# A fused attention and gated-FFN layer on one core: squares of low parts on TensorE, integer weights on SyncE's queue, the first Q stack in two halves

## The chip, the cores and the metric

One core of a Trainium2 chip runs the whole layer for 16 batches in one launch. The metric is the device time of the launch in microseconds. The engines are named as in the profile: PE is TensorE (PEld its weight load), DVE is VectorE, ACT is ScalarE, POOL is GpSimd and SP is SyncE, which here only issues DMAs. A time with a decimal point and no unit is a time in us from the start of the span.

## The reference, cut to what matters

For each of 16 batches (x is 256 queries by 256 channels, ctx 120 rows by 256, 16 heads of depth 16):

```python
def layernorm(x): return (x - mean(x)) / sqrt(var(x) + 1e-5)
Q, K, V = layernorm(x) @ Wq.T + bq, ctx @ Wk.T + bk, ctx @ Wv.T + bv
scores  = einsum('bhqd,bhkd->bhqk', Q, K) * 0.25 / temperature
x = x + einsum('bhqk,bhkd->bhqd', softmax(scores), V) @ Wo.T + bo
n = layernorm(x)
h = silu(n @ (w_gate / 127).T) * (n @ (w_up / 127).T)      # integer weights, hidden 768
x = x + h @ (w_down / 127).T
```

## The kernel before, in words

The kernel keeps float32 accuracy on a matrix engine that rounds its inputs: each operand is a high part and a low part, and a product is three matmuls, high by high, low by high and high by low. Q and K are split into three bf16 parts (high, middle, lowest), and the six products that matter are put below one another as 96 rows of one tile, the Q stack `qs` and the K stack `ks`. SP builds a stack by six DMAs of 16 rows each from the parts that ACT (high, `highest` L509; middle, `middle` L515), DVE (the rest, `rest_of` L636) and POOL (lowest, `third` L457) make; `stack` (L358) issues them. The A group (L894) is the score product from which DVE takes row maxima (`max`, L704); the maxima are transposed (`shift`, L818) and go as two more rows into the Q stack (`shift rows`), and the B group (L904) then gives transposed scores with the maximum subtracted, which ACT exponentiates (L536). `pv` (L920) multiplies by V. Then come the normalisation by row sums, the output product `wo`, the second layernorm, six gate-up products and two down products.

The integer weights are loaded as int32 into the buffers of `y`, `x1` and `x_res`, before these are in use. ACT rounds them into the high part (`integer_weight`, L493), DVE makes the low part (L667). For weights that fit, the low part is all zero, and the products with it are skipped. Whether that is so is found at run time: `look_for_wide` (L417) squares and adds the three low parts on POOL in 512-column pieces, with nine multiplications and eight additions, and halves the sum three times; `tell_if_wide` (L670) reduces it on DVE, a one-column matmul (L883) adds over partitions, DVE writes the answer to a register word (`told`), and PE reads it (`read`). The first `pv` waits for the answer too.

The order of work on each engine is written out beforehand. Time is cut into steps, 32 for a batch. `JOBS` gives PE's work with the step and the PSUM bank, `LAG` all other kinds, `EVERY` the distance of the parts of one kind, `START` work that is done once, and `SHIFT` moves a kind in one batch. Every engine walks through the steps in order and emits what is due; a step takes no time of its own, so only the order on each engine counts, and semaphores do the rest. `WARM` puts matmuls of the identity with itself between PE's work in the head (L880). Every engine runs its own program in order: an instruction that waits holds all behind it, and a DMA issued by SP stands behind every earlier wait of SP. The first layernorm's mean and variance are on DVE (`stats1`, `var1`), its reciprocal root on POOL (`rsqrt`, L439), its application on ACT (`norm_apply`, L521). `ctx` is split into parts by ACT (`ctx hi`) and POOL (`ctx lo`, L474) for two batches at a time, and K is computed for two batches at a time.

Of the kernel before, what the change touches and what calls it, by code (L numbers as in the profile page):

```python
# [13 lines left out]
P = 128  # L14
RING = 3
# [6 lines left out]
    ("k", 0, -59, 3),  # L22
    ("normT1", 0, -56, 1),
    ("q", 0, -51, 1),
    ("v", 0, -45, 0),
    ("shift", 0, 9, 2),
    ("attQ", 0, 56, 3),
    ("attQ", 1, 56, 1),
    ("attT", 0, 61, 3),
    ("wo", 0, 69, 0),  # L30
    ("normT2", 0, 84, 2),
    ("gateup", 0, 87, 2),
    ("gateup", 1, 89, 0),
    ("gateup", 2, 93, 1),
    ("gateup", 3, 97, 2),
    ("gateup", 4, 104, 3),
    ("gateup", 5, 106, 0),
    ("down", 0, 113, 3),
    ("down", 1, 118, 1),
# [7 lines left out]
    "A": -22, "max": -19, "load x_res": -11, "shift rows": -1, "bias x_res": 4, "shift hi": 10, "shift lo": 13,  # L47
    "exp": 21, "B": 21, "pv": 34, "pv copy": 37, "rsum": 57, "att": 58, "attT hi": 62,
    "attT lo": 64, "x1": 72, "stats2": 73, "rsqrt2": 74, "var2": 74, "norm2": 82, "normT2 hi": 83,
    "normT2 lo": 85, "tanh": 88, "gate": 89, "hid": 90, "hid hi": 92, "hid lo": 94, "hid lo last": 111,  # L50
    "y": 117, "store": 157,
}
EVERY = {
    "rsum": 1, "k rows": 4, "q rows": 1, "exp": 4, "A": 4, "B": 4, "max": 4, "pv": 16, "pv copy": 15,
# [5 lines left out]
    "load wv": -115, "load wo": -57, "load bv": -124, "load bo": -29, "weight q": -64, "weight o": -30,  # L60
    "weight v": -42, "ones rows": -44, "load wg": -70, "load wu": -65, "load wd": -73, "int hi": (-42, -26, -24),
    "int lo": (-36, -29, -20), "look": (-30, -26, 6), "tell": 31, "sum": 36, "told": 32, "read": 68,
# [4 lines left out]
    "A": {3: -1, 15: -2},  # L67
    "B": {1: -1},
    "att": {1: -3},
    "attQ": {0: 3, 1: -2},  # L70
    "attT": {0: 3},
    "attT hi": {0: 2},
    "ctx hi": {0: -2},
    "ctx lo": {0: -10, 2: -9},
    "exp": {1: -2},
    "hid lo": {14: 3},
    "k rest": {2: 1},
    "k rows": {2: 1},
    "max": {15: -1},
    "norm1": {3: -5},  # L80
    "normT1": {3: -4},
    "normT1 hi": {3: -4},
    "normT2": {14: -2},
    "pv": {0: 2},
    "pv copy": {1: -1},
    "q mid": {1: 7},
    "q rest": {0: 5},
    "q rows": {2: -3},
    "q third": {15: -17},
    "rsqrt2": {15: -3},  # L90
    "rsum": {1: -4},
    "shift lo": {0: -1, 1: -2},
    "stats1": {2: -6},
    "stats2": {0: 1},
    "wo": {14: -3},
    "x1": {1: 1},
# [47 lines left out]
def build(nc, x, ctx, wqT, bq, wkT, bk, wvT, bv, woT, bo, temp, tempc, wgT, wuT, wdT, out):  # L144
# [27 lines left out]
    with es:  # L172
# [72 lines left out]
        WIDE_LEFT = 64  # L245
        wide_one = tanh_g[:].rearrange("p a q -> p (a q)")
        WIDE_STEPS = 3 * 6 - 1 + 3
# [16 lines left out]
        ks_in = [sem(f"ks_in{r}") for r in range(RING)]  # L264
        shift_in = [sem(f"shift_in{r}") for r in range(RING)]
# [7 lines left out]
        wide_got, wide_all, wide_col, wide_sum, wide_set = sem("wide_got"), sem("wide_all"), sem("wide_col"), sem("wide_sum"), sem("wide_set")  # L273
# [56 lines left out]
        def _(sp):  # L330
# [27 lines left out]
            def stack(kind, n, part, t, dst, arrived, parts):  # L358
# [4 lines left out]
                for r in range(len(parts)):  # L363
                    if parts[r] == part:
                        sp.dma_start(dst[n % RING][r * D:(r + 1) * D], src).then_inc(arrived[n % RING], 16)

            def step(i):
                if i == START["load wv"]:
                    load_weight("v", wvT)
                if i == START["load wo"]:  # L370
                    load_weight("o", woT)
                if i == START["load bv"]:
# [33 lines left out]
        def _(pool):  # L406
# [10 lines left out]
            def look_for_wide(k):  # L417

                pool.wait_ge(gint_lo, k + 1)
                flat = (wg, wu, wd)[k][:, 1].bitcast(F32).rearrange("p c n -> p (c n)")  # L420
                done = 6 * k - (k > 0)
                for part in range(3):
                    piece = flat[:, part * 512:(part + 1) * 512]
                    if k + part == 0:
                        nc.gpsimd.tensor_tensor(wide_sq, piece, piece, ALU.mult).then_inc(wide_got, 1)
                        done += 1
                        continue
                    pool.wait_ge(wide_got, done)
# [537 lines left out]
```

## Time and profile before

| what | value |
|---|---|
| median of 3 runs | 418.03 us (417.88 to 419.41) |
| the profiled execution's own time | 417.83 us |
| its span, first to last instruction | 415.70 us |
| mean granted TensorE clock | 0.967 of full speed |
| PE busy | 376.0 us, 90% of the span |
| DVE, ACT, POOL busy | 299.0, 254.5, 183.0 us |
| chain that ended last, by engine | PE 73%, POOL 11%, DMA, ACT and DVE 4% each |

The share of an engine is over the whole span; the head (until TensorE is busy without a break), the steady turns and the tail have to be read apart. The chain is followed back from the last instruction, at each step to what released it.

### The profile page before, as it was taken

Reading aid. Unit: us, or ns where it says so; the run is one execution under the profiler, and the core shown is the slowest. Engines: PE = TensorE matmul, PEld = TensorE weight load, DVE = VectorE, ACT = ScalarE, POOL = GpSimd, SP = SyncE. Lnnn points to the kernel's source line nnn. Section 1 sums busy time; section 2 is a strip of 40 time slices with the busy share of each in tenths; the row PEclk is TensorE's granted clock in tenths of the full one; section 3 lists DMA queues with packets and bytes.
Section 4 is the critical chain, followed back from the end, with each engine's and each line's share of the span. In section 5 each row is a group of like instructions: output and inputs, shape, how many; then the busy total and the mean of one; then the engine's idle time right before and its main releaser. Section 6 shows DMA issues by size and latency. Waiting matters only on the chain.

```text
span 415.7 us, 9912 instructions
## 1 busy us (share of the span) xinstructions
PE 376.0 (90%) x3492; PEld 338.6 (81%) x3492; DVE 299.0 (72%) x733; ACT 254.5 (61%) x564; POOL 183.0 (44%) x302
## 2 busy tenths in 40 slices
PE   7359567979999999999999999999999999997985
PEld 6359545758998999998999999999999988786974
DVE  6388272678878788778777877787778785745664
ACT  2422244757677767767766766676767665756442
POOL 3139993415544445345452635353444332514223
PEclk9859895999999999999999999999999999999999
DMA  6955445657371737262736264645535451010000
GB/s 149 304 74 129 63 100 102 125 84 115 74 122 41 114 94 120 75 120 75 132 76 123 69 128 87 105 88 114 102 79 90 88 78 54 3 54 2 27 25 27
DMA packets 61700, 37.69 MB, mean 91 GB/s; under 512 B 34000, under 2 KB 61136, under 8 KB 61648
## 3 DMA queue, kind: packets, MB, share of 16 engines
q1 hardware_dynamic: 60320, 34.63, 43.6%
q10 hardware_dynamic: 1328, 2.36, 1.7%
q8 instruction: 33, 0.54, 0.6%
q14 instruction: 19, 0.16, 0.2%
HBM read 14.04 MB, written 4.19 MB: 44 GB/s over the span
## 4 chain that ended last, share of the span: by engine, by line
PE 73%; POOL 11%; DMA 4%; ACT 4%; DVE 4%; issue 2%; SPq 1%; POOLq 0%; ACTq 0%; DVEq 0%
PE ps_w L799 30%; PE ps_w L792 10%; PE ps_o L920 7%; PE ps_b L904 7%; PE ps_a L894 6%; PE ps_w L811 5%; PE ps_w L784 4%; PE ps_w L832 3%; POOL hid L431 3%; DMA x_tok<-x 3%; POOL tanh_g L429 2%; POOL hidT L452 2%; DMA qs<-q 1%; DVE ks L689 1%; ACT xn L521 1%
## 5 line engine op out<-in xcount | busy, mean ns | idle before, releaser
L452 POOL TENSOR_TENSOR hidT<-hid,hidT 128x256 fp32r<-128x256 f32 x80 | 59.0, 738 | 130.5 <-ACT hidT L529 130.5
L799 PE MATMUL ps_w<-xn2T,wg 128*128 128x256 f32 x384 | 102.3, 300 | 0.3 <-DVE xn2T L629 0.2
L704 DVE TENSOR_REDUCE negmax<-ps_a 128x4 f32<-128x480 f32 x128 | 82.7, 650 | 19.9 <-PE ps_a L894 19.9
L799 PE MATMUL ps_w<-xn2T,wu 128*128 128x256 f32 x384 | 95.6, 281 | 0.0
L536 ACT ACTIVATE probs<-ps_b 120x512 f32<-120x512 f32 x128 | 76.1, 594 | 26.6 <-PE ps_b L904 26.3
L799 PEld LDWEIGHTS ps_w<-xn2T,wg 128*128 128x128 f32 x384 | 72.3, 188 | 1.5 <-DVE xn2T L629 0.7
L799 PEld LDWEIGHTS ps_w<-xn2T,wu 128*128 128x128 f32 x384 | 72.6, 189 | 0.0
L799 PE MATMUL ps_w<-wd,hidT 128*128 128x256 f32 x384 | 55.9, 292 | 2.8 <-DVE hid L764 1.5
L547 ACT ACTIVATE tanh_g<-ps_w 128x256 f32<-128x256 f32 x96 | 36.6, 382 | 34.4 <-PE ps_w L799 33.8
L904 PE MATMUL ps_b<-qs,ks 98*120 98x256 bf16 x256 | 51.0, 281 | 3.9 <-ACT probs L536 3.9
L894 PE MATMUL ps_a<-ks,qs 96*128 96x120 bf16 x512 | 49.0, 219 | 4.7 <-DMA qs<-q 3.8
L799 PEld LDWEIGHTS ps_w<-wd,hidT 128*128 128x128 f32 x384 | 48.3, 189 | 5.4 <-DVE hid L764 1.9
L529 ACT ACTIVATE hidT<-hid 128x256 fp32r<-128x256 f32 x96 | 39.7, 414 | 10.7 <-DVE hid L764 10.1
L760 DVE SCALAR_TENSOR_TENSOR hid<-tanh_g,ps_w 128x256 f32<-128x256 f32 x96 | 39.2, 409 | 7.4 <-ACT tanh_g L547 5.4
L894 PEld LDWEIGHTS ps_a<-ks,qs 96*128 96x128 bf16 x512 | 31.8, 99 | 12.2 <-DMA qs<-q 4.3
L764 DVE TENSOR_TENSOR hid<-hid,ps_w 128x256 f32<-128x256 f32 x96 | 39.5, 412 | 1.9
L904 PEld LDWEIGHTS ps_b<-qs,ks 98*120 98x120 bf16 x256 | 27.5, 135 | 12.1 <-issue 6.2
L920 PE MATMUL ps_o<-probs,v_one 120*32 120x256 f32 x512 | 35.1, 393 | 0.6 <-ACT probs L536 0.5
L792 PE MATMUL ps_w<-xn1T,wq 128*128 128x256 f32 x192 | 27.5, 293 | 0.4 <-DVE xn1T L629 0.4
L629 DVE TENSOR_TENSOR xn2T<-ps_w,xn2T 128x512 fp32r<-128x512 f32 x16 | 11.1, 692 | 21.8 <-ACT xn2T L498 21.8
L784 PE MATMUL ps_w<-wv,ctxT 128*120 128x256 f32 x96 | 16.2, 306 | 11.0 <-DVE wv L600 11.0
L792 PE MATMUL ps_w<-wo,attT 128*128 128x256 f32 x192 | 26.0, 284 | 0.0
(94 smaller groups left out, 659.0 us busy)
## 6 DMA issues: line engine op xcount, KB each, us to landing
qs<-q SPq DMA_DIRECT2D x96, 128.0 KB, 4.6
ks<-k SPq DMA_DIRECT2D x96, 60.0 KB, 2.7
x_tok<-x SPq DMA_DIRECT2D x16, 256.0 KB, 3.7
x_res<-x SPq DMA_DIRECT2D x16, 256.0 KB, 3.9
out<-y SPq DMA_DIRECT2D x16, 256.0 KB, 3.2
ctx_raw<-ctx SPq DMA_DIRECT2D x16, 120.0 KB, 2.5
x_res<-wdT ACTq DMA_DIRECT2D x1, 768.0 KB, 9.0
y<-wgT ACTq DMA_DIRECT2D x1, 768.0 KB, 10.9
```

Of the source, the lines that this page charges most:

```text
L452: nc.gpsimd.tensor_tensor(hidT[:, 1, f], hid[:, f % 2], hidT[:, 0, f].bitcast(F32), ALU.subtract).then_inc(hid_lo, 1)
L529: nc.scalar.activation(hidT[:, 0, f], hid[:, f % 2], ACT.Copy).then_inc(hi["hid"], 1)
L536: nc.scalar.activation(probs[0:NKV, e % PROBS], ps_b[0:NKV], ACT.Exp).then_inc(exp_done, 1)
L547: nc.scalar.activation(tanh_g[:, f % 2], bank_of("gateup", f)[:, 0:NQ], ACT.Tanh, scale=DEQ / 2).then_inc(tanh_done, 1)
L704: nc.vector.tensor_reduce(negmax[:, n % RING, qt, h0:h0 + AG], ps_a[ga % 2][:, 0:AG * NKV].rearrange("p (h k) -> p h k", h=AG), AX.X, ALU. ...
L760: nc.vector.scalar_tensor_tensor(hid[:, f % 2], tanh_g[:, f % 2], 1.0, ps[:, 0:NQ], ALU.add, ALU.mult).then_inc(gated_done, 1)
L764: nc.vector.tensor_tensor(hid[:, f % 2], hid[:, f % 2], ps[:, NQ:2 * NQ], ALU.mult).then_inc(emptied["gateup"], 1)
L792: last = nc.tensor.matmul(dst, lhsT, rhs, start=(k == 0 and one is sums[0]), stop=(k == len(one) - 1), skip_group_check=True)
L799: last = nc.tensor.matmul(dst, lhsT, rhs, start=(start and k == 0), stop=(stop and k == len(terms) - 1), skip_group_check=True)
L894: last = nc.tensor.matmul(ps_a[ga % 2][:, k * NKV:(k + 1) * NKV], qs[n % RING][0:KS_ROWS, h0 + k, qt * P:(qt + 1) * P], ks[n % RING][0:KS_ ...
L904: last = nc.tensor.matmul(ps_b[0:NKV, k * NQ:(k + 1) * NQ], ks[n % RING][:, gb * HG + k], qs[n % RING][:, gb * HG + k], start=True, stop=True)
L920: last = nc.tensor.matmul(ps_o[k % HQ * VW:(k % HQ + 1) * VW, k // HQ], v_one[n % RING][:, h], probs[0:NKV, count(n, GROUPS, h // HG) % PR ...
```

## The change

- `look_for_wide` on POOL goes. In its place PE multiplies each 128-column piece of the three low parts with itself and adds all 36 products in one PSUM tile; the diagonal holds sums of squares. They are issued in six pieces of six. DVE multiplies the tile by the identity and takes the maximum of each row (L672 and what follows, as before).
- The filler matmuls (`WARM`) go.
- The three integer weights are loaded from SP's queue, each in two halves (by chunks), in place of ACT's queue.
- For batch 0 each of the six Q rows is sent as two DMAs of 128 queries, the first with a semaphore of its own, `qs_half_in`; the A groups of the first 128 queries (four of eight) wait for that one alone.
- The step tables are written anew: nearly all lags move by six steps, which changes no order by itself; kinds move against each other by one to nine steps in all batches, and by more in batches 0 to 3 and 13 to 15. The second transpose goes from bank 2 to bank 3, the first down product from bank 3 to bank 2. On POOL the residual's bias (`bias x_res`) goes from between the low parts of the hidden tile to behind the second layernorm's root.

```diff
-    ("normT2", 0, 84, 2),
+    ("normT2", 0, 89, 3),
-    ("down", 0, 113, 3),
+    ("down", 0, 119, 2),
...
-    "A": -22, "max": -19, "load x_res": -11, "shift rows": -1, "bias x_res": 4, "shift hi": 10, "shift lo": 13,
+    "A": -16, "max": -13, "load x_res": -6, "shift rows": 14, "shift hi": 16, "shift lo": 19, "bias x_res": 24,
...
-    "weight v": -42, "ones rows": -44, "load wg": -70, "load wu": -65, "load wd": -73, "int hi": (-42, -26, -24),
-    "int lo": (-36, -29, -20), "look": (-30, -26, 6), "tell": 31, "sum": 36, "told": 32, "read": 68,
+    "weight v": -51, "ones rows": -133, "load wg": (-57, -50), "load wu": (-47, -46), "load wd": (-42, -40), "int hi": (-46, -29, -21),
+    "int lo": (-36, -25, -18), "squares": (-20, -19, -15, -14, -11, -9), "tell": -3, "sum": 2, "told": 7, "read": 61,
...
+    "norm1": {0: -44, 1: -4, 3: -15},
+    "q mid": {0: 7, 1: -2, 2: 1, 3: 2, 13: -2, 15: -3},
+    "q rows": {0: -3, 1: 4, 2: 6, 3: 5, 13: -4, 15: -3},
+    "q third": {0: -5, 1: 4, 2: 3, 3: -2, 13: -1, 14: 6, 15: 4},
+    "rsqrt1": {0: -70, 1: 4, 3: -3, 13: 8},
+    "var1": {0: -64, 1: -2, 2: -5, 3: -12},
...
-WARM = {-59: 10, -56: 2, -51: 5, -40: 12, -24: 4, -22: 18, -18: 2, -14: 2, -10: 2, -6: 2, -2: 2, 2: 2, 6: 2}
-FIRST, LAST = -142, TURN * (BATCHES - 1) + 204
+FIRST, LAST = -225, TURN * (BATCHES - 1) + 235
...
+            def load_integers(k, half):
+                w, chunks, arrived = ((wgT, CC, gate_in), (wuT, CC, up_in), (wdT, FC, down_in))[k]
+                part = slice(half * chunks // 2, (half + 1) * chunks // 2)
+                sp.dma_start(raw_int[k].rearrange("p (c n) -> p c n", c=chunks)[:, part], w.rearrange("(c p) n -> p c n", p=P)[:, part]).then_inc(arrived, 16)
...
-                    if parts[r] == part:
+                    if parts[r] == part and kind == "q" and n == 0:
+                        for half in range(QT):
+                            sp.dma_start(dst[0][r * D:(r + 1) * D, :, half * P:(half + 1) * P], src[:, :, half * P:(half + 1) * P]).then_inc(qs_half_in if half == 0 else arrived[0], 16)
+                    elif parts[r] == part:
...
+                if kind == "q" and n == 1:
+                    act.wait_ge(qs_half_in, 6 * 16)
...
-                dve.wait_ge(wide_got, WIDE_STEPS)
-                nc.vector.reduce_max(wide_any[:], wide_sq[:, 0:WIDE_LEFT], AX.X).then_inc(wide_all, 1)
+                dve.wait_ge(wide_squares, 6)
+                dve.wait_ge(ident_done, 2)
+                nc.vector.tensor_tensor(wide_sq[:, 0:P], ps_o[:, 0, 0:P], ident[:], ALU.mult).then_inc(wide_diag, 1)
+                dve.wait_ge(wide_diag, 1)
+                nc.vector.reduce_max(wide_any[:], wide_sq[:, 0:P], AX.X).then_inc(wide_all, 1)
...
+            def squares_of_low_parts(piece):
+                w = (wg, wu, wd)[piece // 2][:, 1].rearrange("p c n -> p (c n)")
+                pe.wait_ge(gint_lo, piece // 2 + 1)
+                for k in range(6):
+                    part = w[:, (piece % 2 * 6 + k) * P:(piece % 2 * 6 + k + 1) * P]
+                    last = nc.tensor.matmul(ps_o[:, 0, 0:P], part, part, start=(piece == 0 and k == 0), stop=(piece == 5 and k == 5), skip_group_check=True)
+                last.then_inc(wide_squares, 1)
...
+                    if ga == 0 and n == 0:
+                        pe.wait_ge(qs_half_in, 6 * 16)
+                    if ga == (GROUPS // QT if n == 0 else 0):
+                        pe.wait_ge(qs_in[n % RING], slot_count(n, 1, 1) * (6 * 16))
```

## Rows read from the trace of the kernel before

**Rows 1.** Busy by stage: stretch, length, PE, PEld, DVE, ACT, POOL, clock, DMA, GB/s.
```profile
37.00:48.00 11.00, 6.99 (x74) 6.75 (x72) 6.29 (x15) 1.96 (x4) 10.39 (x9) 1.00 0.58 90
60.00:72.00 12.00, 8.52 (x56) 5.53 (x57) 4.71 (x11) 5.34 (x10) 5.53 (x10) 0.58 0.64 117
186.70:229.55 42.85, 42.85 (x424) 39.19 (x428) 34.25 (x89) 30.69 (x72) 19.72 (x35) 1.00 0.51 99
```

**Rows 2.** TensorE's waits, 37 to 100: total us, times, longest.
```profile
PE ps_w L784 <- POOL ctxT L474: 4.2, 1, 4.2
PE ps_a L894 <- DMA qs<-q: 3.8, 2, 2.6
PE ps_w L811 <- ACT xn L521: 2.9, 1, 2.9
```

**Rows 3.** Busy by stage for POOL alone: stretch, length, busy, clock, DMA, GB/s.
```profile
30.08:46.85 16.77, 15.92 (x11) 0.96 0.69 120
51.90:60.87 8.97, 8.34 (x9) 1.00 0.41 92
```

**Rows 4.** Timeline of PE: start, us, what; the score groups that open batches 0 to 3.
```profile
37.19 0.38 PE L894 MATMUL ps_a<-ks,qs 96*128 96x120 bf16 x4
...
54.45 0.38 PE L894 MATMUL ps_a<-ks,qs 96*128 96x120 bf16 x4 [1.24 <-DMA qs<-q]
...
69.83 0.60 PE L894 MATMUL ps_a<-ks,qs 96*128 96x120 bf16 x4
...
87.59 0.38 PE L894 MATMUL ps_a<-ks,qs 96*128 96x120 bf16 x4 [2.57 <-DMA qs<-q]
```

**Rows 5.** Groups of DVE, 0 to 40: busy, mean ns, idle before.
```profile
L689 DVE MEMSET ks<- 2x1920 bf16 x3 | 5.0, 1658 | 1.2 <-issue 1.2
```

**Rows 6.** Timeline of several engines: durations that the sum uses.
```profile
5.75 0.43 SPq L335 DMA_DIRECT2D probs<-wvT  x1
...
7.68 2.89 PE L784 MATMUL ps_w<-ctxT,wk 128*128 128x240 f32 x12 [1.52 <-POOL ctxT L474]
...
9.20 1.09 ACT L521 ACTIVATE xn<-x_tok,norm_bias,rstd 128x256 f32<-128x256 f32 x2 [3.02 <-POOL norm_bias L447]
...
13.14 1.66 PE L792 MATMUL ps_w<-xn1T,wq 128*128 128x256 f32 x12 [0.39 <-DVE xn1T L629]
...
17.06 1.48 ACT L493 ACTIVATE wg<-y 128x1536 fp32r<-128x1536 int32 x1 [0.89 <-DMA y<-wgT]
...
24.73 0.28 POOL L442 TENSOR_TENSOR minus_mean<-zero_col,meanvar 128x2 f32<-128x2 f32 x1 [7.39 <-DVE meanvar L648]
...
26.34 0.20 POOL L447 TENSOR_TENSOR norm_bias<-minus_mean,rstd 128x2 f32<-128x2 f32 x1
...
27.23 1.16 POOL L457 TENSOR_TENSOR q<-q_rest,q 128x512 bf16<-128x512 f32 x1 [0.70 <-ACT q L515]
27.88 2.13 DVE L667 TENSOR_TENSOR wg<-y,wg 128x1536 fp32r<-128x1536 int32 x1
...
32.51 3.88 SPq L365 DMA_DIRECT2D ks<-k  x6
...
49.37 1.16 POOL L457 TENSOR_TENSOR q<-q_rest,q 128x512 bf16<-128x512 f32 x1
...
70.59 2.41 PE L792 MATMUL ps_w<-xn1T,wq 128*128 128x256 f32 x12
```

**Rows 7.** DMA issues, whole span: count, KB each, median us to landing.
```profile
qs<-q SPq DMA_DIRECT2D x96, 128.0 KB, 4.6
ks<-k SPq DMA_DIRECT2D x96, 60.0 KB, 2.7
```

**Rows 8.** Groups of PE by form, whole span.
```profile
L880 PE MATMUL ps_o<-ident 128*128 128x128 f32 x130 | 21.6, 329 | 1.5 <-POOL ident L409 1.5
```

**Rows 9.** Chain that ended last, in order of time: start, us, what.
```profile
341.94 1.37 POOL x_res L480 x2
```

**Rows 10.** TensorE's waits, 330 to 416.
```profile
PE ps_w L811 <- ACT xn L521: 2.5, 3, 1.2
```

More of the change, by code:

```diff
@@ L63 @@
+    "int lo": (-36, -25, -18), "squares": (-20, -19, -15, -14, -11, -9), "tell": -3, "sum": 2, "told": 7, "read": 61,
 }
 SHIFT = {
[L67 to L82, printed above, removed]
@@ L83 @@
-    "normT2": {14: -2},
-    "pv": {0: 2},
[L85 to L96, printed above, removed]
-}
-WARM = {-59: 10, -56: 2, -51: 5, -40: 12, -24: 4, -22: 18, -18: 2, -14: 2, -10: 2, -6: 2, -2: 2, 2: 2, 6: 2}
-FIRST, LAST = -142, TURN * (BATCHES - 1) + 204
+    "A": {0: 5, 1: 1, 3: -1, 15: -3},
@@ new lines @@
+    "B": {0: -2},
+    "attQ": {13: -1},
+    "attT": {0: 1, 13: 2, 14: 3, 15: -2},
+    "attT hi": {0: -1, 3: -1, 13: 2, 14: 3, 15: 1},
+    "attT lo": {1: 3, 2: -2, 13: 3, 14: -1},
+    "bias x_res": {0: -16, 1: 17, 2: 4, 13: 10},
+    "ctx hi": {0: -53, 1: 17, 2: -2, 3: -3, 13: 6},
+    "ctx lo": {0: -60, 1: -20, 2: -8, 3: 13, 13: 8},
+    "down": {14: -2, 15: 15},
+    "exp": {0: -1, 1: -1, 13: 1},
+    "gate": {15: 23},
+    "hid": {2: 1, 13: 1, 15: 25},
+    "hid hi": {14: 2, 15: 23},
+    "hid lo": {0: -1, 1: -1, 3: -1, 13: -10, 14: -2, 15: 3},
@@ new lines @@
+    "hid lo last": {14: 6, 15: 31},
[6 rows of a table added]
+    "load ctx": {0: -62, 1: -16, 2: -9, 3: -20, 13: 11},
+    "load x": {0: -70, 1: -6, 2: -26, 3: -31, 13: 2, 14: -16},
+    "load x_res": {0: 13, 2: 8, 13: 18, 15: -13},
+    "max": {0: 1, 1: -1, 2: -1, 15: -2},
[18 rows of a table added]
+    "rsum": {13: -1},
+    "shift": {0: 2, 1: -1, 2: 2, 13: 2},
+    "shift hi": {0: 9, 1: 1, 2: 1, 3: 2, 13: 1},
+    "shift lo": {2: 2, 13: 1},
+    "shift rows": {0: 9, 1: -1, 2: -4, 13: 3, 14: 6, 15: 6},
+    "stats1": {0: -91, 1: -29, 2: -8, 3: -13, 13: -2},
@@ L371, in step @@
                     load_weight("o", woT)
+                for k, name in enumerate(("load wg", "load wu", "load wd")):
+                    if i in START[name]:
+                        load_integers(k, START[name].index(i))
                 if i == START["load bv"]:
@@ L415, in _ @@
             pool.wait_ge(consts_done, 1)
[L417 to L428, printed above, removed]
-                    nc.gpsimd.tensor_tensor(wide_one, piece, piece, ALU.mult).then_inc(wide_got, 1)
-                    pool.wait_ge(wide_got, done + 1)
-                    nc.gpsimd.tensor_tensor(wide_sq, wide_sq, wide_one, ALU.add).then_inc(wide_got, 1)
-                    done += 2
-                if k == 2:
-                    for half in (256, 128, 64):
-                        pool.wait_ge(wide_got, done)
-                        nc.gpsimd.tensor_tensor(wide_sq[:, 0:half], wide_sq[:, 0:half], wide_sq[:, half:2 * half], ALU.add).then_inc(wide_got, 1)
-                        done += 1
             def rsqrt(which, n, got, eps_sem, out_sem, norm_sem):
@@ L716, in step @@
                     dve.wait_ge(emptied["wo"], count(n, 1, 1))
+                    at_least(dve, var2, count(n - 1, 1, 1))
                     norm_stats(1, x1[:, n % RING], n, stats2)
@@ L722, in step @@
                     dve.wait_ge(x_in[n % RING], slot_count(n, 1, 1) * 16)
+                    at_least(dve, var1, count(n - 1, 1, 1))
                     norm_stats(0, x_tok[:, n % RING], n, stats1)
@@ L876, in _ @@
             wide = []
+            def squares_of_low_parts(piece):
[5 more added lines that the diff above has]
+                last.then_inc(wide_squares, 1)
             def step(i):
-                for _ in range(WARM.get(i, 0)):
-                    nc.tensor.matmul(ps_o[:, 1, 0:P], ident[:], ident[:], start=True, stop=True)
+                if i in START["squares"]:
+                    squares_of_low_parts(START["squares"].index(i))
                 if i == START["sum"]:
                     pe.wait_ge(wide_col, 1)
-                    nc.tensor.matmul(ps_o[0:1, 0, 0:1], wide_any[:], ones_col[:], start=True, stop=True).then_inc(wide_sum, 1)
+                    nc.tensor.matmul(ps_o[0:1, 1, 0:1], wide_any[:], ones_col[:], start=True, stop=True).then_inc(wide_sum, 1)
                 if i == START["read"]:
```

71 lines of the change are left out of this document (34 added, 37 removed), and 24 rows, old and new, of tables (LAG, SHIFT).

## The prediction

> **What bounds the kernel now.** I read the busy table by stages first, because a share over the whole span mixes three regimes. In two steady turns, 186.70 to 229.55, TensorE is busy for all of their 42.85 us at the full granted clock [rows 1]: 21.43 us a batch, and sixteen of them would be 342.8 us. The span is 72.9 us longer, and that lies before the steady part and behind it. No edit that only reorders engines other than TensorE can gain anything in between. In the head TensorE works 6.99 of 11.00 us and 8.52 of 12.00 us [rows 1], and the first of these stretches includes matmuls on the identity (L880) that compute nothing.
>
> Then I asked whom TensorE waits for in the head [rows 2]: 4.2 us for the low part of ctx, which POOL makes, 3.8 us for Q stacks to land, 2.9 us for ACT's normalisation, which in turn needs POOL's reciprocal root. The third view shows what POOL does then: the scan for wide weights holds it from 30.08 to 46.85 and again from 51.90 to 60.87, 24.3 us of work in 20 instructions [rows 3]. POOL works in program order, so the ctx low part, the root for batch 2 and the third part of Q for batch 1 stand behind the first scan, and the third part of K and the root for batch 3 behind the second. The head is bound by a scan that nobody needs before the first PV product. TensorE's milestones set the scale [rows 4]: first score groups of batches 0 to 3 at 37.19, 54.45, 69.83 and 87.59.
>
> **The change, part by part.** I add up the profiled execution, span 415.70, its own time 417.83 (2.13 us around the span; the median of the runs, 418.03, is 0.2 above it).
>
> *Start until the first score group.* The three memsets of ones rows move from between Q's high part and Q's rest to ahead of the first variance. They are 5.0 us of work with 1.2 us before them, 6.2 us in all [rows 5]. So the first normalisation on ACT, at 9.20 before, starts near 9.2 + 6.2 = 15.4, some 0.4 sooner because POOL's root now stands ahead of the ctx low part: 15.0. It takes 1.09, the transposes, copies and the K product follow in a row (2.89 us for K's twelve matmuls at their slow first speed) and K's high part is out near 20.5. Then ACT has the first integer weight (1.48), K's middle part and Q's high part (to 23.5), the second integer weight (to 25.0); DVE makes the first low part (2.13) and then the second batch's variance, near 24.4. POOL's root takes 1.8 (24.73 to 26.54 in the row), ACT's normalisation of batch 1 ends near 27.3, and only then comes Q's middle part (to 27.9), since ACT has it behind that normalisation. POOL's third part takes 1.16: 29.1, against 28.39 before (durations and starts in [rows 6]). The memsets thus gain nothing here: what they free at Q's rest is spent at the front.
>
> Then SyncE's queue. An issue of such rows costs 0.65 us (3.88 for six), one of a weight 0.43 [rows 6], and batch 0 has twelve Q issues in place of six: 3.9 us more of queue. In order from 20.5: three of K, two weights, two of K, one weight (near 25.0), six of Q's high part (29.0; its middle part has been ready for a us), four of the middle part, one of K, and the first half of the lowest part, out near 32.8. A half is 64 KB in runs of 256 bytes; no such transfer is in the trace. The nearest row is K's, 60 KB in runs of 240 bytes, 2.7 us; the whole Q rows take 4.6 [rows 7]. Nothing makes a half slower than the whole, so 2.7 to 4.6; I take 3.3, near K's. Scores of batch 0 start near 36.1, 1.1 us earlier than 37.19. The halves are issued alternately, so the early semaphore saves only the last issue, 0.65 us, and the wait for the second half is hidden behind the four groups before it.
>
> Here the skill has a rule against the change: the Trainium skill, "DMA: Bandwidth & Descriptors", section "Rules for kernel authors", advises against cutting one transfer in two, since both halves go through the same engines, and its section "Specifications" wants 512 bytes or more in a transfer for full rate. K's rows agree in part: a 240-byte transfer of half the size takes more than half the time. By the rule a pair of halves costs 2 x 2.7 - 4.6 = 0.8 us more than a whole, and the forecast would be 408.8.
>
> The integer weights move to SyncE's queue, six issues in place of three on ACT. Four of them and two of x sit before the K rows, while SyncE has nothing else to do until 20.5; hidden. The two of the last weight and the output weight stand between K's and Q's rows, 3 x 0.43 = 1.3 us, and 1.1 of it is on the path above, since Q's middle part comes at 27.9 and the queue is free at 29.0. What stays tied to them is the low part of the last weight, which the fifth squares piece needs ahead of the first scores: the load is out near 25.0, down 4 us later by Q's row, then ACT 1.48 and DVE 2.13, so 32.7. That is 3.4 us before 36.1: covered.
>
> *Squares on TensorE.* 36 matmuls of 128x128. The identity matmuls of that shape are 130 instructions, two for each, 21.6 us [rows 8]. Bounds: 0.06 us each, half of a 256-column matmul in the Q product (1.66 for twelve [rows 6]), or 0.33, two identity instructions as they overlapped; 2 to 12 us in all. I take 0.14 for each, the row per column nearest to it in type: 5 us. Four of six pieces run while TensorE waits for DVE; two, 1.7 us, lie around the first scores and the first Q product of batch 1. They replace 65 identity matmuls, so TensorE's load falls. DVE gains one product over 128 columns, between 0 and 1 us (POOL's over 512 columns take 1.16), and a sum of it is not late: the second batch's Q stack, not the last maxima, releases that batch. The telling is done by 45, well ahead of the first PV.
>
> *POOL free.* This is the gain. The ctx low part of batch 2 now waits for its load (SyncE issues it near 34) and ACT: near 39.6, instead of after the first scan's end at 46.85 [rows 3]. The third part of Q for batch 1 ends near 42.6 instead of 50.53 (its row starts at 49.37), so its stack lands near 47.8, and the first scores of batch 1 start 6.7 us earlier than 54.45 [rows 4, 6]. From there the path is Q product, high, rest, middle (ACT has two exponentials first), third, 0.65 issue, 4.6 landing: batch 2's scores near 62.3, 7.5 earlier. The root for batch 3, which stood behind the second scan's end at 60.87, is done by 51, so the 2.9 us wait for ACT goes too. What is late next is again the Q stack, behind the exponentials on ACT. For batch 3 I get 77.8 (9.8 earlier), as the order puts its third part behind only the ctx low part and one root. From then on TensorE has gate-up work to fill every wait, as in the steady row. Head: 9.8 us; I take off 1.3 for semaphore hops not counted and for the first matmuls without filler: 8.5.
>
> *Steady turns.* Kinds move by one or two places. The bank of the second transpose goes to 3 and that of the down product to 2: the gate-up product must now wait for the first y. It is covered by the second down half (twelve matmuls, as Q's 1.66) with PV, V and a transpose besides, against one short DVE instruction. I take 0, from -1 to +10.
>
> *Tail.* The residual's bias moves from between the low parts to behind the root: 1.37 us of POOL leaves the path twice (at 341.94, and again one turn on [rows 9]), but TensorE waits only 2.5 us for that normalisation in three places, one of them 1.2 [rows 10]. So the two give back at most 2.5 - 1.2 = 1.3: I take 1.3.
>
> Sum: 417.83 - 8.5 - 1.3 = 408.0.
>
> **Rivals.**
> 1. *TensorE's clock without filler.* In the stretch from 60 to 72, behind a 2.9 us wait, the granted clock is 0.58 (1.2 GHz for most of it), and twelve Q matmuls take 2.41 against 1.66 us [rows 1, 6]. The change removes all 65 filler matmuls, which also stand in the gaps between batch 0's score groups, where the clock was 1.00. For it: the gaps stay. Against: the maxima on DVE, not TensorE, pace the scores. I count some 38 us of dense work (the two full Q, K, V and score sets and half a turn of gate-up) between 36 and 92; at 1.45 times (2.41 / 1.66) that is 17 us more, of which the idle 18 us hide most. Three tenths on the path give back 5: 413. The skill's rule stands beside it: the Trainium skill, "TensorE: Matmul & The Clock Gate", Part 1, says the throttled state is the default and only activity lifts it; the row of 60 to 72 agrees.
> 2. *SyncE's queue takes POOL's place.* Twelve halves, K rows, shift rows and loads stand in one in-order queue; each wait there holds all behind it. If a Q or shift issue of batches 1 and 2 comes 3 us late each, 6 are lost: 414. For it: 3.8 us of stack waits already [rows 2]. Against: all twelve halves are out by 33.5, before batch 1 needs the queue.
> 3. *Slower: the exchanged banks stall every turn.* Place: the gate-up product behind the first y, in 14 turns. From 0.7 us a turn the gain is gone (14 x 0.7 = 9.8); at 1.1 it is 423.4. For it: steady turns have no slack on TensorE at all [rows 1]. Against: the cover named above.
>
> **How the numbers follow.** Forecast 0.57 (own range 402 to 412), clock 0.18, queue 0.14, banks 0.06, anything else 0.05. The low end, 400.0, has two thirds of the scan's 24.3 us leave the path (16.2) with the tail's 1.3; the high end, 415.5, takes in rivals 1 and 2 and the upper bound of the squares (7 us more, of which a fifth lies on the path). Half a per cent, 2.1 us, is about what can be told from no change. Faster 0.87 (forecast, clock, most of queue, part of the rest), same 0.05, slower 0.08 (banks and part of the rest).
>
> **What would show it.** Right: POOL's scan rows gone and the third part of batch 1's Q before 44; first scores near 36, 48, 62 and 78; steady pairs of turns still 42.85; the first two waits for ACT's normalisation in the tail gone. Wrong: scores of batch 0 later than 38 (squares or queue), slow matmuls past 60 (clock), any TensorE wait in a steady turn (banks), Q stack waits over 6 us in the head (queue).

## The result and the profile after

The changed kernel takes 415.53 us (median of 20 runs, 412.63 to 418.87) against 418.25 for the kernel before (20 runs, 413.95 to 421.13). The ratio is 0.9945, 95% interval 0.992 to 0.9969: faster by half a per cent, 2.3 us by the ratio, where 10 had been forecast. The profiled execution took 413.98 us (span 412.2); the forecast was set against 417.83, so 3.85 us came where 9.83 were expected.

The busy table by stages, columns as in [rows 1], the first and last of its stretches again and one between them:

```profile
37.00:48.00 11.00, 7.38 (x60) 6.75 (x60) 4.58 (x13) 3.85 (x8) 3.60 (x6) 0.75 1.01 136
60.00:72.00 12.00, 9.43 (x93) 7.18 (x92) 5.13 (x10) 5.71 (x12) 1.04 (x1) 0.87 0.79 110
186.70:229.55 42.85, 42.85 (x424) 39.17 (x424) 34.44 (x88) 30.89 (x70) 19.41 (x34) 1.00 0.56 106
```

The steady part is what it was, TensorE busy for all of 42.85 us. POOL's scan is gone; the same stretches as in [rows 3], for POOL alone:

```profile
30.08:46.85 16.77, 3.50 (x6) 0.63 1.17 117
51.90:60.87 8.97, 4.65 (x8) 0.69 0.51 99
```

POOL's work there fell from 24.3 to 8.2 us. The last two figures of a line are the share of the DMA engines and GB/s: in the first stretch the share rose from 0.69 to 1.17 while the rate stayed (120, now 117). The share adds up the times of all packets; above 1, packets of one engine overlap in time. Now the score groups that open batches 0 to 3, as in [rows 4]:

```profile
39.24 0.58 PE L919 MATMUL ps_a<-ks,qs 96*128 96x120 bf16 x4 [3.46 <-DMA qs<-q]
...
52.29 0.58 PE L919 MATMUL ps_a<-ks,qs 96*128 96x120 bf16 x4 [1.87 <-DMA qs<-q]
...
67.34 0.38 PE L919 MATMUL ps_a<-ks,qs 96*128 96x120 bf16 x4 [1.42 <-DMA qs<-q]
...
84.63 0.39 PE L919 MATMUL ps_a<-ks,qs 96*128 96x120 bf16 x4 [2.60 <-DMA qs<-q]
```

All four wait for a Q stack. Batch 0 starts 2.05 us later than before, batches 1 to 3 start 2.16, 2.49 and 2.96 earlier; the second PV half of batch 2 starts at 98.16 (100.92 before). So the head gives 2.76 us, the rest of the span 0.74 and the time around the span 0.35, in all 3.85.

TensorE's waits from 37 to 100 (total, times, longest), and then the one from 320 on that answers to [rows 10]:

```profile
PE ps_a L919 <- DMA qs<-q: 9.3, 4, 3.5
PE ps_a L919 <- DVE negmax L716: 2.2, 3, 1.4
```
```profile
PE ps_w L825 <- ACT xn L536: 0.4, 1, 0.4
```

The waits for POOL's ctx and ACT's normalisation in [rows 2] are gone; the waits for Q's landing went from 3.8 to 9.3 us. The chain of waits of the changed kernel tells where batch 0's stack comes from (start, us, what; a DMA's time counts from the start of its issue):

```profile
14.62 1.10 ACT xn L536 x2
...
19.29 0.82 ACT k L524 x2
20.13 0.71 SPq L399
...
31.89 0.62 SPq L399
32.55 6.64 DMA qs<-q
39.24 0.58 PE ps_a L919 x4
```

From 20.13, when K's high part is out, SyncE issues without a pause until 33.83. The third part of Q is ready at 27.96 and its halves are issued at 32.55 and 33.2: it stands almost five us in the queue, and then takes over six to land.

### The profile page after: what moved, and what is told of

Its sections match the earlier page's. It is cut to its first block, busy times and chain, and to the rows that moved or that the text cites. A ratio compares the mean times of both kernels' runs of the same rounds, so it can differ in the third digit from the quotient of the medians.

```text
span 412.2 us, 9745 instructions
## 1 busy us (share of the span) xinstructions
PE 363.0 (88%) x3398; PEld 326.1 (79%) x3398; DVE 299.6 (73%) x734; ACT 255.7 (62%) x564; POOL 157.4 (38%) x282
## 4 chain that ended last, share of the span: by engine, by line
PE 74%; DMA 8%; SPq 5%; POOL 4%; ACT 4%; DVE 3%; issue 2%; POOLq 0%; ACTq 0%; DVEq 0%
PE ps_w L813 30%; PE ps_w L806 10%; PE ps_o L945 7%; PE ps_b L929 6%; PE ps_a L919 6%; DMA qs<-q 6%; PE ps_w L798 5%; PE ps_w L825 5%; PE ps_w L846 3%; SPq L399 3%; DMA x_res<-x 2%; SPq L397 1%; ACT probs L551 1%; DVE ks L701 1%; POOL hidT L467 1%
## 5 line engine op out<-in xcount | busy, mean ns | idle before, releaser
L919 PE MATMUL ps_a<-ks,qs 96*128 96x120 bf16 x512 | 50.2, 222 | 12.5 <-DMA qs<-q 10.1
L919 PEld LDWEIGHTS ps_a<-ks,qs 96*128 96x128 bf16 x512 | 30.8, 100 | 21.0 <-DMA qs<-q 11.2
L825 PE MATMUL ps_w<-ident,xn 128*128 128x128 f32 x128 | 20.8, 288 | 16.2 <-ACT xn L536 16.2
L487 POOL TENSOR_TENSOR ctxT<-ctx_raw,ctxT 128x480 fp32r<-128x480 f32 x8 | 9.7, 1216 | 51.7 <-ACT ctxT L590 51.7
L806 PE MATMUL ps_w<-xn1T,wq 128*128 128x256 f32 x192 | 29.2, 305 | 0.0
L825 PEld LDWEIGHTS ps_w<-ident,xn 128*128 128x128 f32 x128 | 15.0, 147 | 17.5 <-issue 17.5
```

Of the source, the lines that this page charges most:

```text
L806: last = nc.tensor.matmul(dst, lhsT, rhs, start=(k == 0 and one is sums[0]), stop=(k == len(one) - 1), skip_group_check=True)
L825: last = nc.tensor.transpose(ps[:, c * NQ + t * P:c * NQ + (t + 1) * P], src[:, t, c * P:(c + 1) * P], ident[:])
L919: last = nc.tensor.matmul(ps_a[ga % 2][:, k * NKV:(k + 1) * NKV], qs[n % RING][0:KS_ROWS, h0 + k, qt * P:(qt + 1) * P], ks[n % RING][0:KS_ ...
```

## Experiments

Each ratio is to the kernel before, run on the same chip; the changed kernel's own is 0.9945 (0.992 to 0.9969).

**Whole rows, clock, memsets, scan alone.** Theory: batch 0's halves and SyncE's queue ate the gain. Rivals: the clock without filler; the memsets at the front; a scan that was worth less than forecast.

*e1: whole Q rows in batch 0, as before the change.*

```
-  if parts[r] == part and kind == "q" and n == 0: (two halves)
-  elif parts[r] == part:
+  if parts[r] == part:
```

> The changed kernel with the Q rows of batch 0 sent whole (six DMAs, one semaphore), all else as changed. Theory Q (the stack of batch 0 is late because twelve halves double the packets and the issues in the DMA queue): first scores at 36.0 to 37.5 in place of 39.24, DMA share above 1.2 for some 6 us less, the ctx load of batch 2 lands some 2 us sooner, and the time falls by 1.5 to 3 us to some 413. Rival C (TensorE's low clock took the gain): first scores may come sooner, but the Q product of batch 1 still takes 2.9 us and the time changes by less than 0.5 us. The prediction's own step (a half lands as fast as a K row, 3.3 us): first scores 0 to 1 us later than with halves.

413.12 us, ratio 0.9879 (0.9845 to 0.9912). First scores at 36.15 and 47.99, 3.1 and 4.3 earlier than in the changed kernel. The halves cost 0.7% as sent. The end of batch 0's chain in this run:

```profile
29.40 6.70 DMA qs<-q
36.10 0.05 issue
36.15 0.38 PE ps_a L912 x4
```

The last whole row takes as long to land as the last half did (6.70 and 6.64). The gain lies in the issue: with six issues fewer it goes out at 29.40 in place of 32.55.

*e2: identity matmuls in the head's waits.* 39 of them, into a bank that is free.

```
+  for _ in range(k):
+      nc.tensor.matmul(ps_b[:, 0:P], ident[:], ident[:], start=True, stop=True)
```

> The changed kernel with filler matmuls of the identity put back into TensorE's waits of the head (24 ahead of the third squares piece and of the first scores, 15 between the later score groups up to batch 1's second). Theory C (low clock): the Q products of batches 1 and 2 fall from 2.91 to 1.7 us, first scores of batch 1 at 51 and of batch 2 at 65 to 66, the time falls by 1.5 to 2.5 us. Theory Q (DMA queue): the two Q products are faster but first scores stay at 39.2, batch 1's fall by no more than 1.2 and the time by 0 to 1 us.

414.58 us, 0.9898 (0.9872 to 0.9923), at most half a per cent from the changed kernel, with intervals that touch. The stretch from 24 to 56 of the changed kernel, then of this one (columns as in [rows 1]):

```profile
24.00:56.00 32.00, 19.14 (x126) 17.57 (x125) 18.25 (x36) 9.08 (x17) 8.76 (x15) 0.63 1.06 133
```
```profile
24.00:56.00 32.00, 22.61 (x210) 21.08 (x208) 18.57 (x37) 9.98 (x19) 9.16 (x16) 1.00 1.06 133
```

The granted clock went from 0.63 to 1.00, the twelve matmuls of batch 1's Q product from 2.91 to 1.68 us, and the first scores of the four batches came at 39.54, 52.29, 66.62 and 84.61: nowhere as much as one us earlier. The clock was low, and it was not on the path to the first scores of these batches. Whether the half per cent in the total is real, and where it would come from, is not shown.

*e3: the memsets of ones rows late.*

```
-  "ones rows": -133
+  "ones rows": -13
```

> The changed kernel with the three memsets of ones rows moved from ahead of the first variance to where DVE is idle before the first maximum (step -13). Start theory (the chain from the first layernorm to SyncE's rows is on the path, memsets and all): ACT's first normalisation at 9 instead of 14.6, K rows issued from 14.5 instead of 20.1, first scores 3 to 5 us earlier than 39.24 and the time 2 to 4 us lower. Rival (what is late is the load of the last integer weight and the squares that stand ahead of the first scores, or DMA packets): first scores at most 1 us earlier, time within 1 us.

409.02 us, 0.9771 (0.9738 to 0.9803): 1.7%, 7.3 us, better than the changed kernel. Its chain and its first score group:

```profile
8.21 1.10 ACT xn L536 x2
...
14.02 0.71 SPq L399
```
```profile
30.95 0.39 PE L919 MATMUL ps_a<-ks,qs 96*128 96x120 bf16 x4 [1.75 <-DMA qs<-q]
```

Set beside the chain above, the normalisation moves by 6.4 us, K's first row on the queue by 6.1, the first scores by 8.3.

*e4: before, with only the scan replaced by the squares* (and nine of the eighteen filler matmuls at their place taken out).

```
-  if i in START["look"]: look_for_wide(...)
+  SQUARES = {-22: (0, 1), -18: (2,), -14: (3,), -10: (4,), -6: (5,)}
```

> The kernel before with one part of the change alone: POOL's scan replaced by the squares on TensorE and the diagonal on DVE, the fillers ahead of the first scores halved from 18 to 9, tables otherwise as before (whole Q rows, integer weights on ACT's queue). The prediction's theory (the scan is what bounds the head): batch 1's first scores near 47, the time 6 to 9 us below before. Theory Q (behind the scan SyncE's queue and the stacks' landing come next): the ctx low part at 41 to 43 in place of 46.9, batch 1's first scores at 49 to 51, the time 2 to 4 us below before. If it is as fast as the changed kernel, the other parts of the change gave nothing together.

414.70 us, 0.9874 (0.9832 to 0.9915). First scores at 37.09, 50.04, 65.01 and 83.17, against [rows 4] 0.1, 4.4, 4.8 and 4.4 earlier. This one part gives more than the whole change; the others together cost 0.7%, with the nine fillers counted to the scan.

**POOL's order, and the queue's load.** In the changed kernel POOL waits long for the residual's load, ahead of a root:

```profile
53.91 1.42 POOL L493 TENSOR_TENSOR x_res<-x_res,bo_row 128x256 f32<-128x256 f32 x2 [6.96 <-DMA x_res<-x]
```

*e5: that bias later.*

```
-  "bias x_res": {0: -16, 1: 17, 2: 4, 13: 10}
+  "bias x_res": {0: 17, 1: 17, 2: 4, 13: 10}
```

> The changed kernel with one place moved: POOL adds batch 0's residual bias behind the root of batch 3 and the low part of batch 2's K, where it stood ahead of them and waited 7.0 us for its load. Theory 'POOL's order': the wait holds everything behind it on POOL, so batch 2's scores come up to 2.5 us earlier than 67.3 and batch 3's 2 to 4 us earlier than 84.6; total 1 to 3 us less than the changed kernel. Theory 'stacks' (SyncE's queue and the landing of Q decide each batch): scores move less than 1 us, total within 0.8 us of the changed kernel.

415.68 us, 0.9983 (0.995 to 1.0015): no gain. The third part of batch 2's Q starts at 59.56 (59.88 in the changed kernel), as it waits for ACT's middle part:

```profile
59.56 1.16 POOL L472 TENSOR_TENSOR q<-q_rest,q 128x512 bf16<-128x512 f32 x1 [3.89 <-ACT q L530]
```

The wait for the residual stands on the chain of waits, but another stands right behind it that ends nearly as late. 'POOL's order' falls. The program up to batch 0's first scores is the changed kernel's here, and they came at 38.48 in place of 39.24: differences of that size between two profiles say nothing.

*e7: integer weights on ACT's queue.*

```
-  sp.dma_start(raw_int[k]..., part)
+  act.dma_start(raw_int[k]..., part)
```

> The changed kernel with the six loads of integer weights back on ACT's queue. Theory 'issues' (the queue in program order is the limit): three issues of 0.5 to 0.65 us go from between K's and Q's rows, first scores 1 to 2 us earlier than 39.2, total 0.5 to 2 us less. Theory 'short runs' (the DMA engines are the limit while 240 and 256-byte runs are moved): the last half still lands near 39, total within 0.8 us of the changed kernel.

418.98 us, 1.0046 (1.0011 to 1.0082): slower, which neither theory had. On ACT the issues stand behind its own waits: the first four, out by 9.67 on SyncE, come between 19.61 and 21.45, when K's rows go out too. The last weight's two halves then take 8.9 us to land (median), K's rows pause on SyncE (22.72, then 26.05), and the first scores come at 43.56. The move to SyncE, at these places in the order, is worth 1.0%.

**Why the halves land late.**

*e8: batch 0's halves by rows of the stack.*

```
-  dst[0][r*D:(r+1)*D, :, half*P:(half+1)*P], src[:, :, half*P:(half+1)*P]
+  dst[0][r*D + half*D//2 : r*D + (half+1)*D//2], src[half*P//2 : (half+1)*P//2]
```

> The changed kernel with the twelve Q issues of batch 0 cut by rows of the stack, not by queries: as many issues and the same bytes, but runs as long as those of the whole rows; the scores then wait for all twelve. Theory 'short runs': 64 KB land in 3 to 4.6 us in place of 6.6, first scores at 36.5 to 37.5, total 2 to 4 us less. Theory 'issues': twelve issues end where they did (33.8), landing 4 us or more, first scores at 38 or later, total within 1 us of the changed kernel.

416.40 us, 0.9975 (0.9933 to 1.0017). First scores at 41.89 with a wait of 5.89 us: long runs alone do not help. It is no clean test, though: the share of the DMA engines from 28 to 36 is only 0.65 to 0.69 while the stack lands later than in the changed kernel, so part of the engines seem to have had no work from it.

*e11: halves by heads.*

```
+  dst[0][r*D:(r+1)*D, half::CC], src[:, half]
```

> The changed kernel with the twelve Q issues of batch 0 cut by heads, not by queries: as many issues and the same bytes, in runs of 512 bytes over all sixteen rows of a part; the scores wait for all twelve. Theory 'packets' (256-byte runs double the packets, and a packet costs the engines about the same): share of the DMA engines from 28 to 36 us near 1.2 in place of 1.4, landing 4 to 5 us after the last issue at 33.8, first scores near 38.2, total 0.5 to 1.5 us less than the changed kernel. Theory 'issues': first scores at 39 or later, as with halves by queries.

414.01 us, 0.9917 (0.9885 to 0.9949). As many issues, ended at 33.82, and first scores at 36.37: as with whole rows (36.15), whose last issue ended at 30.03. The issues are those of the changed kernel, so the 2.9 us are landing alone; that is more than 'packets' had forecast. Whole rows and halves by heads come to the same time by different ways: six issues fewer with 6.7 us to land, or twelve issues with 3.1 for the last. In the total this run cannot be told from the changed kernel.

*e9: output weight and last integer weight loaded early.*

```
-  "load wo": -44, "load wd": (-42, -40)
+  "load wo": -49, "load wd": (-48, -47)
```

> The changed kernel with the loads of the output weight and of the last integer weight ahead of K's rows on SyncE's queue, into the stretch from 16 to 20 us in which the DMA engines move nothing. Theory 'burst' (Q's rows come late because weights, K's rows and Q's rows all pass the DMA engines between 22 and 38 us): 1.0 MB leaves that burst, three issues of 0.5 to 0.6 us leave the queue, first scores at 35 to 37.5 in place of 39.2, total 2 to 4 us less than the changed kernel. Theory 'packets' (the 256-byte runs alone keep the engines busy): Q's last issues end 1.2 to 1.7 us sooner, first scores at 37.5 to 38.5, total 1 to 2 us less.

412.26 us, 0.9877 (0.9823 to 0.9931). First scores at 36.01, as 'burst' had it. The first half sent lands in 3.1 us; in the changed kernel, behind the last integer weight, it took 5.7.

*e13: all first halves ahead of all second halves; nothing else.*

```
-  for half in range(QT):
-      sp.dma_start(... half * P:(half + 1) * P ...)
+  sp.dma_start(... 0:P ...)
...
+  if kind == "q" and n == 0 and part == 2:
+      for r in range(len(parts)):
+          sp.dma_start(... P:2 * P ...)
```

> The changed kernel with one thing moved: batch 0's six first halves ahead of its six second halves, where the change sends both halves of a row one behind the other; as many issues, bytes and runs of 256 bytes. Theory 'same rows' (two transfers to the same sixteen rows at once slow each other): DMA share from 28 to 36 us at 0.6 or less in place of 1.4, halves land in 2.7 to 3.5, first scores at 33 to 36. Theory 'burst' (weights and rows together fill the engines, the order does not matter): share still over 1.1, halves 5 us or more, first scores 38 or later. In both the load of ctx goes out no sooner than before, so batch 1 gains at most 2 us and the total 1 to 3 us less than the changed kernel under 'same rows', within 1.5 us under 'burst'.

414.09 us, 0.9917 (0.9878 to 0.9956): in the total not to be told from the changed kernel. First scores at 35.77, and they do not wait for the stack at all, but for the squares ahead of them. By that the scores cannot tell the theories apart: the order also sends the sixth first half at 29.46 in place of 32.55. The landing can: the second halves go out between 30.12 and 34.05 and land in 2.7 to 3.0 us, where the halves sent at that time in the changed kernel take 6.4 to 6.6. 'Same rows' holds for the landing, and for the share from 32 on. Batch 1 gains 1.7 us. Now the stretches 28 to 32 and 32 to 36 side by side (the last two figures: share of the DMA engines, GB/s), with the row of the halves (KB each, median us to landing) between 15 and 45. The changed kernel:

```profile
28.00:32.00 4.00, 2.37 (x11) 2.37 (x12) 1.95 (x2) 1.48 (x1) 0.00 (x0) 0.50 1.40 102
32.00:36.00 4.00, 3.78 (x19) 3.59 (x17) 2.65 (x4) 0.60 (x1) 0.00 (x0) 0.50 1.43 84
```
```profile
qs<-q SPq DMA_DIRECT2D x12, 64.0 KB, 6.3
```

First halves first (e13), then halves by heads (e11):

```profile
28.00:32.00 4.00, 2.18 (x11) 2.18 (x11) 2.15 (x2) 1.49 (x1) 0.15 (x1) 0.50 1.10 150
32.00:36.00 4.00, 4.00 (x23) 4.00 (x22) 2.63 (x4) 0.60 (x1) 0.00 (x0) 0.50 0.60 111
```
```profile
qs<-q SPq DMA_DIRECT2D x12, 64.0 KB, 3.2
```
```profile
28.00:32.00 4.00, 2.16 (x11) 2.16 (x11) 2.52 (x2) 1.48 (x1) 0.17 (x1) 0.50 1.17 143
32.00:36.00 4.00, 3.25 (x20) 3.10 (x18) 2.33 (x4) 0.60 (x1) 0.00 (x0) 0.71 0.79 127
```
```profile
qs<-q SPq DMA_DIRECT2D x12, 64.0 KB, 4.2
```

In the changed kernel the packets' times add up to the most and the fewest bytes move. The same twelve transfers in another order land in half the time. Here is what one transfer of batch 0's stack took to land:

| run | least, median, most (us) |
|---|---|
| changed kernel, halves in pairs | 5.7, 6.3, 6.6 |
| e5, the same up to here | 5.2, 5.7, 6.0 |
| e3, the same six us earlier | 4.3, 4.8, 5.3 |
| e9, pairs, fewer loads around them | 3.1, 4.1, 4.5 |
| e11, by heads | 3.1, 4.2, 4.9 |
| e13, six first halves | 3.4, 4.0, 4.6 |
| e13, six second halves | 2.7, 2.8, 3.0 |
| e1, whole rows | 5.6, 6.0, 6.7 |

Two things add up. The delay begins with the weights: the second half of the last weight, issued right ahead of the Q rows, takes 5.5 us, and the first half of Q behind it 5.7; without these loads that is 3.1 (e9). Then the delay is worked off or not. With the halves apart it falls from 4.6 to 2.7, by heads from 4.9 to 3.1; with the halves in pairs it rises from 5.7 to 6.6, and in e9 from 3.1 to 4.5 (in e3 it falls, but only from 5.3 to 4.3; why is not shown), and with whole rows, of twice the bytes, from 5.6 to 6.7. So neither the count, nor the 256-byte runs, nor the weights in the burst are enough alone: pairs of short transfers to the same sixteen rows, one right behind the other, are moved too slowly to make good the delay that they meet. Whether it is the same rows, or 256-byte pieces that lie beside each other in them, and whether on the side that reads or the side that writes, was not separated.

**Versions.**

*e6: whole rows, the bias of e5, and the memsets on POOL, which is idle from 9 to 17.*

```
+  pool.wait_ge(ctx_lo, 1)
+  for r in range(RING):
+      nc.gpsimd.memset(ks[r][KS_ROWS:], 1.0).then_inc(k_ones_set, 1)
+      pool.wait_ge(k_ones_set, r + 1)
```

> The changed kernel with three edits: batch 0's Q rows sent whole, the three memsets of ones rows on POOL, which is idle from 9 to 17 us, and the residual bias of batch 0 later on POOL. If the three costs are separate (halves 3 us, memsets 7, and the 5.7 us that the memsets still hold the first maxima when DVE makes them late, of which up to 3 show), first scores at 28 to 30, batch 1 near 42, total 400 to 405. If they share one limit (SyncE's in-order queue behind the thirds of Q), no less than the 409.0 of the kernel with late memsets alone, less 1.

406.71 us, 0.9764 (0.9716 to 0.9811); first scores at 30.14 and 43.27. The first scores are at the end of the first theory's range, but by the ratio the total cannot be told from e3's (0.9771), which has the late memsets alone. That is what 'one limit' had: the 0.7% of the whole rows does not come on top. The first scores come only 0.8 us earlier than in e3: the last Q row goes out at 23.28, where e3's last first half went out at 26.43, but it takes 6.8 us to land in place of 4.5.

*e10: e6 with the early loads of e9.*

> The kernel with whole Q rows, ones rows on POOL and the later bias, and with the same early loads. Theory 'burst': the whole rows land in 4 us in place of 6, first scores at 27 to 29 in place of 30.1, total 403 to 405.5 against 406.7. If K and Q themselves fill the engines, no change: within 1 us of 406.7.

406.01 us, 0.974 (0.9688 to 0.9793), the lowest median of all; not to be told from e3 or e6, though the first scores come 1.0 us sooner than in e6. Its score groups of batches 0, 1 and 3:

```profile
29.14 0.62 PE L913 MATMUL ps_a<-ks,qs 96*128 96x120 bf16 x4
...
42.26 0.58 PE L913 MATMUL ps_a<-ks,qs 96*128 96x120 bf16 x4 [1.72 <-DMA qs<-q]
...
74.04 0.58 PE L913 MATMUL ps_a<-ks,qs 96*128 96x120 bf16 x4 [2.80 <-DMA qs<-q]
```

Batch 0 no longer waits for its stack, so whole rows leave nothing for halves to win. Its chain now runs through the load of the second integer weight (its second half is issued at 10.71 and takes 8.6 us to land) and the squares.

*e12: e10 with halves, first halves first.*

> The kernel with ones rows on POOL, later bias and early loads, with batch 0's Q stack in halves again, but now all six first halves ahead of all six second halves. If the early semaphore is worth something once the order serves it: half the bytes ahead of the first scores, first scores at 27 to 28 in place of 29.1, total 1 to 2 us less than 406.0. If short runs eat it (1536 packets of 256 bytes for the first halves against 768 of 1 KB for the whole rows): first scores at 29 or later, the fifth group waits for the second halves to 34 or later, total 406 to 409.

408.79 us, 0.9817 (0.9754 to 0.988). Halves land in 2.7 us and scores start at 28.39, but the six second halves stand ahead of ctx on SyncE's queue, and K's product of batch 1 waits:

```profile
35.27 2.89 PE L801 MATMUL ps_w<-ctxT,wk 128*128 128x240 f32 x12 [3.93 <-POOL ctxT L494]
```

*e14: e12 with ctx between the first and second halves.*

> The kernel with first halves ahead of second halves, ones rows on POOL, later bias and early loads, with the two loads of ctx between the first and the second halves. If the 3.9 us wait for ctx's low part was the whole price of the halves: batch 1 at 41 to 42.3, total 403.5 to 406, no slower than the kernel with whole rows (406.0). If the six extra issues hold up batch 1's K rows and x as well: batch 1 at 43 or later, total 406.5 to 408.5.

408.67 us, 0.9777 (0.9726 to 0.9827). The wait for ctx is gone, but batch 1's Q rows are all issued only by 39.66 (37.72 in e10) and its scores come at 45.36 (42.26). ACT may not write batch 1's Q before the second halves have left the buffer:

```profile
32.86 0.84 ACT L531 ACTIVATE q<-ps_w,bq_col 128x256 bf16<-128x256 f32 x2 [3.49 <-DMA qs<-q]
```

Here the issues count: the second halves stand ahead of something else, on the queue or in the buffer. By the profiles e12 and e14 start batch 0 0.7 us earlier than e10 and batch 1 2.9 to 3.1 later; the totals' intervals overlap with e10's. The 0.7 us are not shown to be the halves': none of the three waits for its stack there, and the last six squares ahead of the scores take 0.83 us in e12 and e14 against 1.48 in e10, where the granted clock was still 0.50.

## Why the prediction was wrong

*What was right:* the sign and the mechanism, a scan that POOL did for nobody; the first normalisation (15.0 forecast, 14.62 measured), K's high part (20.5; 20.13), the end of the queue (all halves out by 33.5; 33.83) and the steady turns (42.85). For the tail 1.3 was forecast, and the span behind the head gives 0.74. The signs that the prediction had named point at the queue of stacks: scores of batch 0 later than 38 (39.24) and stack waits over 6 us in the head (9.3). The third part of batch 1's Q, due before 44, began at 45.80.

*The step that failed* is the landing of batch 0's halves: "2.7 to 4.6; I take 3.3". The half that releases the first scores was out at 33.17, where 32.8 was forecast, and landed 6.0 us later. So of the 3.1 us by which the first scores missed 36.1, 0.4 is queue (the three weight issues alone took 1.7 us for 1.3) and 2.7 landing. The ground was "Nothing makes a half slower than the whole". A half did not take longer than a whole row at the same place (e1: 5.6 to 6.7), but it took about as long, and the bound of 4.6 was wrong for both: it is a median over the whole span [rows 7]. The same trace has batch 0's own whole rows, in the head, at up to 6.1 us:

```profile
L365 SPq DMA_DIRECT2D qs<-q x6: 552/600/615, 18.1 to 28.4; - x6
DMA to landing us min/median/max: 3.3/4.9/6.1
```

What decided was what is ahead of a transfer and right behind it on the queue: the weights' loads, and then the pairs. The forecast also read [rows 7] as counted from the end of an issue, though it counts from the start; this made each landing about 0.6 us longer than the row says, and hid a part of the miss. The rule of the Trainium skill weighed there ("DMA: Bandwidth & Descriptors", section "Rules for kernel authors") speaks of halves by partitions. It pointed the right way for halves by queries too, but the 0.8 us worked out beside it was too little: e1 gives 3.1 at the first scores, and by fewer issues, not by a shorter landing.

It is luck that e1 agrees with the forecast's first two milestones (36.15 and 47.99 for 36.1 and 47.8): it has six issues fewer than the forecast counted and a landing twice as long.

*The second*: the memsets "gain nothing here". The chain was argued through Q's middle part, ready at 27.9, behind the normalisation of batch 1. In the trace that part was on time (the third was done at 27.96, forecast 29.1), and the path was the other one, the queue that starts with K's high part. The forecast had both within 1.1 us of each other and took the cost of one as covered by the other. Late memsets give 7.3 us (e3): with an in-order queue as the path, whatever delays its first entry costs in full. This did not move the forecast's time, which counted the memsets ahead of the first normalisation; what it missed is what leaving them late would have been worth.

*The third* is the scan's worth. Without it batches 1 to 3 were to gain 5.6, 6.4 and 8.7 us on batch 0 (the forecast's gains less its 1.1); in e4 they gain 4.3, 4.7 and 4.3. Batch 3 was credited with most and got no more than batch 1. In the changed kernel what came next was again the landing of Q's rows, 5.7 us from the end of its last issue (78.97 to 84.63) where 4.6 had been taken from the median.

In the profiled pair: 3.1 at batch 0, and 3.7 more until batch 3 (5.0 gained on batch 0 in place of 8.7), less the 1.3 that had been taken off, makes 5.5 of the 5.7 us that the head lacks (2.76 in place of 8.5).

*Rivals.* The clock was low as rival 1 said (0.63 from 24 to 56), but raising it brought no first scores a whole us earlier, and the total moved by half a per cent or nothing (e2). Rival 2, the queue in POOL's place, was right in kind: all four batches wait for stacks. But it put the price at batches 1 and 2 and held batch 0 safe, since "all twelve halves are out by 33.5". They nearly were (33.83), but out is not landed, and batch 0 lost 3.1 us. Rival 3 is false: no wait in the steady part. The squares took 6.9 us for the 5 forecast:

```profile
L897 PE MATMUL ps_o<-wu 128*128 128x128 f32 x12 | 2.9, 411 | 4.8 <-DVE wu L676 4.8
L897 PE MATMUL ps_o<-wd 128*128 128x128 f32 x12 | 2.4, 356 | 0.0
L897 PE MATMUL ps_o<-wg 128*128 128x128 f32 x12 | 1.6, 280 | 2.0 <-DVE wg L676 2.0
```

They stand beside 6.8 us of waits for DVE, as forecast. The last six squares ahead of the first scores end at 35.8, so a stack that landed sooner would have waited for them, as e13's did (35.77). Two slips in the sums change nothing: 417.83 - 16.2 - 1.3 is 400.3, not 400.0, and half of a 256-column matmul of the Q product is 0.07, not 0.06.

## What to carry to other kernels

Where a chain runs through an in-order queue, look for the first entry of its unbroken run of issues: what delays that entry costs in full, and what delays a later one may cost nothing. A bundle of edits can hide a loss: one edit alone (the scan, 1.3%) gave more than all together (0.55%), and moving the memsets by one number gave 1.7% on top. Gains do not add up: whole rows gave 0.7% in the changed kernel and nothing that could be told once the memsets were out of the way. A landing time for a new kind of transfer is bounded from above only by a row with the same neighbours on the queue, not by a larger transfer's median.

## What the runs showed of the hardware

Twelve 64 KB transfers with 256-byte runs, sent in pairs to the same sixteen rows, kept the DMA engines at a share of 1.40 to 1.43 while they moved 84 to 102 GB/s, and landed in 6.3 us (5.7 in e5, 4.8 in e3 and 4.1 in e9, with the same order); the same transfers, with the pairs apart (e13), ran at 1.10 and 0.60 with 150 and 111 GB/s and landed in 3.2 us. Whole rows of 128 KB at that place took 5.6 to 6.7 us (e1). An issue on SyncE's queue took 0.6 to 0.7 us for sixteen rows; on the chain of the changed kernel such issues, with three weight loads among them, follow each other without a pause from 20.13 to 33.83. Halves by partitions (e8) left the share at 0.65 to 0.69, and the last of them took 8.3 us on the chain. A memset of two rows by 1920 bf16 elements held DVE for 1.66 us, and POOL for 1.75 (e10). TensorE's granted clock rose from 0.63 to 1.00 with filler over 32 us of the head (e2), and the first scores of none of the first four batches came as much as one us earlier.
